# Cross-attention of a fused decoder layer: the SyncE queue takes the softmax denominators before the next keys, and the first pass puts its wide maximum pairs in two banks of the scores

## The reference

```python
q_hk = (hidden_q @ Wq.T).reshape(Bv, Sv, H, K)
q_big = jnp.einsum('bshk,hkq->bshq', q_hk, w_kc_q)
q_big = _apply_rope(q_big, sin_q[None, :, None, :], cos_q[None, :, None, :])
kv_r = _apply_rope(kv_c, sin_k[None], cos_k[None])
q_r = jnp.einsum('bshq,hqr->bhsr', q_big, W_qr)
k_r = jnp.einsum('bld,hdr->bhlr', kv_r, W_kr)
scores = jnp.einsum('bhsr,bhlr->bhsl', q_r, k_r)
attn = jax.nn.softmax(scores, axis=-1)
ctx_c = jnp.einsum('bhsl,bld->bhsd', attn, kv_r)
ctx_lat = jnp.einsum('bhsd,hkd->bhsk', ctx_c, w_kc_kv)
ctx = ctx_lat.transpose(0, 2, 1, 3).reshape(Bv, Sv, H * K)
return ctx @ Wo.T
```

## Time and profile before

| | |
|---|---|
| median of 3 runs | 2580.51 us (2574.94 to 2581.4) |
| the profiled execution | 2568.1 us, its span 2566.3 us |
| mean granted TensorE clock over the span | 0.961 |
| busy over the span | PE 2317.2 us (90%), PEld 1447.2 us (56%), DVE 1686.8 us (66%), ACT 1189.1 us (46%), POOL 1839.7 us (72%) |
| PE busy in 40 slices of the span, tenths | 7989858999985999999999999999999999999398 |
| PEclk in the same slices | 9999978999996999999999999999999999999699 |

### The profile page before, as it was taken

The page is one execution under the profiler, slowest core; times in us unless marked ns, Lnnn a source line. Parts: engine busy times, 40 slices in busy tenths (PEclk is TensorE's granted clock), DMA queues, the critical chain, the costliest instruction groups (busy, mean ns, idle before and its releaser), DMA issues. The chain is left out here.

```text
span 2566.3 us, 47308 instructions
## 1 busy us (share of the span) xinstructions
PE 2317.2 (90%) x15394; PEld 1447.2 (56%) x15394; DVE 1686.8 (66%) x2816; ACT 1189.1 (46%) x1925; POOL 1839.7 (72%) x827
## 2 busy tenths in 40 slices
PE   7989858999985999999999999999999999999398
PEld 4455446777752555555555555555555555555288
DVE  6888857888855666666666666666666666661475
ACT  3232222232222555655655655655655655664143
POOL 2445526989871888888888788888888888889111
PEclk9999978999996999999999999999999999999699
DMA  4000016666654233333333333333333332320111
GB/s 132 14 24 20 13 51 179 185 175 181 177 161 94 64 78 72 85 80 70 83 75 71 86 70 76 86 73 73 86 75 72 86 77 69 86 64 20 39 45 39
DMA packets 229954, 212.21 MB, mean 83 GB/s; under 512 B 115542, under 2 KB 204842, under 8 KB 229760
## 3 DMA queue, kind: packets, MB, share of 16 engines
q1 hardware_dynamic: 229888, 211.37, 32.5%
HBM read 128.17 MB, written 59.48 MB: 73 GB/s over the span
## 5 line engine op out<-in xcount | busy, mean ns | idle before, releaser
L1670 POOL TENSOR_TENSOR x_acc<-x_acc,x_prob 120x1600 f32<-120x1600 f32 (+1 forms) x320 | 1151.4, 3598 | 54.9 <-ACT x_prob L1691 34.2
L1691 ACT ACTIVATE x_prob<-x_scores 120x800 f32<-120x800 f32 (+1 forms) x768 | 601.5, 836 | 19.3 <-PE x_scores L1864 12.3
L1884 PE MATMUL x_context<-x_prob,x_kv 120*64 120x400 f32 (+1 forms) x3072 | 605.7, 515 | 0.0
L1785 DVE TENSOR_REDUCE x_mx<-x_ring 115x2 f32<-115x1024 f32 (+1 forms) x352 | 431.5, 1226 | 52.8 <-PE x_ring L1927 35.3
L1711 ACT COPY x_half<-x_ring 115x420 f32<-115x420 f32 (+2 forms) x320 | 171.5, 536 | 403.4 <-PE x_ring L1934 403.4
L1794 DVE TENSOR_REDUCE x_mx<-x_ring 115x1 f32<-115x420 f32 (+2 forms) x320 | 197.8, 618 | 222.2 <-PE x_ring L1934 222.2
L1884 PEld LDWEIGHTS x_context<-x_prob,x_kv 120*64 120x64 f32 (+1 forms) x3072 | 187.2, 136 | 260.9 <-issue 260.4
L1864 PE MATMUL x_scores<-x_qh,x_dh 64*120 64x400 f32 (+1 forms) x1536 | 274.0, 352 | 1.0 <-ACT x_prob L1691 0.2
L1864 PE MATMUL x_scores<-x_ql,x_dh 64*120 64x400 f32 (+1 forms) x1536 | 266.7, 342 | 0.0
L1864 PE MATMUL x_scores<-x_qh,x_dl 64*120 64x400 f32 (+1 forms) x1536 | 266.5, 342 | 0.0
L1670 POOL TENSOR_TENSOR x_acc<-x_prob 121x1600 f32<-121x1600 f32 x32 | 115.5, 3609 | 173.3 <-ACT x_prob L1691 173.3
(11 more groups left out here) (176 smaller groups left out, 3659.2 us busy)
## 6 DMA issues: line engine op xcount, KB each, us to landing
x_rden<-scratch_rden SPq DMA_DIRECT2D x68, 200.0 KB, 3.5
scratch_qh<-q_qsh SPq DMA_DIRECT2D x64, 200.0 KB, 3.9
scratch_ql<-q_qsl SPq DMA_DIRECT2D x64, 200.0 KB, 3.8
x_qm<-scratch_qh SPq DMA_DIRECT2D x64, 200.0 KB, 4.2
x_qh<-scratch_qh SPq DMA_DIRECT2D x64, 200.0 KB, 3.4
x_ql<-scratch_ql SPq DMA_DIRECT2D x64, 200.0 KB, 3.8
scratch_kr<-q_krot SPq DMA_DIRECT2D x32, 363.0 KB
x_kr<-scratch_kr SPq DMA_DIRECT2D x32, 363.0 KB
```

Of the source, the lines that this page charges most:

```text
L1670: pool.tensor_tensor(acc[0:rows, parity], first, prob[0:rows, c % PR], ALU.add).then_inc(acc_done.sem, 1)
L1691: act.activation(prob[0:rows, c % PR, u * HALF:(u + 1) * HALF].rearrange("p (j s) -> p j s", j=2), psc[0:rows, u, :, 0:BANK], ACT.Exp).the ...
L1785: dve.tensor_reduce(best[0:block_rows(r), :, r, i], ring[0:block_rows(r), :, 0:b - a], AX.X, ALU.max).then_inc(read_sem(u), 1)
L1884: mm = pe.matmul(pav[DC * s:DC * s + DC, j, 0:BANK], kv[0:rows, parity, c], prob[0:rows, c % PR, cols], start=c == 0, stop=c == LC - 1)
```

## The change

There are two parts.

In SyncE's queue `invert(n)` moves ahead of `load_kr(n + 2)`, in all slots that load keys (-1 to 29); `load_qm` stays in front of both. In the other slots nothing changes.

In the first pass the wide pairs go to `psc[:, 0]`, banks 2 and 3 in the numbering of the new `cells`, instead of the ring. `earlier` takes the banks from `cells` and looks back over up to two slots. Two waits are added: the scores of step 0 in slot 0 wait for the last wide maximum of the first pass, and in the first pass the wide pairs with i == 2 (steps 5 to 11), which read the last third of the keys, wait for turn 2. The output product of the first pass takes one head pair instead of eight.

```diff
@@ -1311,6 +1311,10 @@
         self.first = self.count(first, {})
         self.count([u for n, u in last_units], self.last_where, last_units)
 
+    def cells(self, n, u):
+
+        return (2, 3) if u[0] == "max" and is_at(n, -1) else self.banks[u]
+
     def reader(self, u):
         return 2 if u[0] == "max" else self.banks[u][0]
 
@@ -1344,17 +1348,21 @@
     def earlier(self, n, u):
 
         found, seen = [], []
-        for b in self.banks[u]:
+        for b in self.cells(n, u):
             if isinstance(n, int) and n >= self.last:
                 keys = [(self.last - 1, v) for v in self.units] + list(self.last_where)
                 place = keys.index((n, u))
                 m, v = next(key for key in reversed(keys[:place]) if b in self.banks[key[1]])
+            elif isinstance(n, int):
+                keys = [(m, v) for m in (n - 2, n - 1, n) for v in self.units]
+                place = keys.index((n, u))
+                m, v = next((key for key in reversed(keys[:place]) if b in self.cells(*key)), (None, None))
             else:
                 place = self.units.index(u)
                 before = [(0, v) for v in self.units[:place]]
                 back, v = next(key for key in reversed([(1, v) for v in self.units] + before) if b in self.banks[key[1]])
                 m = n - back
-            if v not in seen:
+            if v not in seen and v is not None:
                 seen.append(v)
                 found.append(self.release(m, v))
         return found
@@ -1610,8 +1618,10 @@
                     store_x2(n - 2, parity)
                 if further:
                     load_qm(n + 2, parity)
+                    invert(n)
                     load_kr(n + 2)
-                invert(n)
+                else:
+                    invert(n)
                 if not last:
                     double_steps(n + 1, 1 - parity)
                     load_m(n + 1, 1 - parity)
@@ -1782,7 +1792,8 @@
                 u = ("max", r, i)
                 wait_filled(dve, n, u)
                 a, b = keys_of(r, i)
-                dve.tensor_reduce(best[0:block_rows(r), :, r, i], ring[0:block_rows(r), :, 0:b - a], AX.X,
+                src = psc[:, 0] if is_at(n, -1) else ring
+                dve.tensor_reduce(best[0:block_rows(r), :, r, i], src[0:block_rows(r), :, 0:b - a], AX.X,
                                   ALU.max).then_inc(read_sem(u), 1)
 
             def half_maximum(n, u):
@@ -1855,6 +1866,8 @@
                 cols = slice(u * BANK, (u + 1) * BANK)
                 halves = [slice(DC * j, DC * j + DC) for j in range(2)]
                 pe.wait_ge(exp_done.sem, exp_done.at(n, 2 * c + u - 1))
+                if is_at(n, 0) and c == 0 and u == 0:
+                    wait_read(pe, n - 1, last_max)
                 if c == 0 and u == 0:
                     pe.wait_ge(q_loaded.sems[parity], q_loaded.done(n, parity))
                     pe.wait_ge(steps_doubled.sems[parity], steps_doubled.done(n, parity))
@@ -1914,17 +1927,21 @@
                         mm = pe.matmul(ring[DC * s:DC * s + DC, bank, 0:BANK], ones[0:LP], acc[:, 1 - parity, cols],
                                        start=True, stop=True)
                 elif u[0] == "out":
-                    for h in range(H // 2):
+                    heads = H // 2 if not is_at(n, -1) else 1
+                    for h in range(heads):
                         if h % 4 == 0:
                             wait(pe, ctx_normed.sem, ctx_normed.at(n, h // 4 + 1))
                         mm = pe.matmul(ring[0:S, bank, 0:E], ctxn[:, h // 4, (h % 4) * S:(h % 4 + 1) * S],
-                                       wco[:, h], start=h == 0, stop=h == H // 2 - 1)
+                                       wco[:, h], start=h == 0, stop=h == heads - 1)
                 elif u[0] == "max":
                     r, i = u[1:]
                     a, b = keys_of(r, i)
+                    dst = psc[:, 0] if is_at(n, -1) else ring
+                    if is_at(n, -1) and i == 2:
+                        wait_read(pe, n, ("turn", 2))
                     for t in range(2):
                         part = slice(DC * t, DC * t + DC)
-                        mm = pe.matmul(ring[0:block_rows(r), t, 0:b - a],
+                        mm = pe.matmul(dst[0:block_rows(r), t, 0:b - a],
                                        qm[part, 1 - parity, r * MR:r * MR + block_rows(r)], kh[part, a:b],
                                        start=True, stop=True)
                 elif u[0] == "half":
```

## The result

The changed kernel takes **2492.88 us** (median; 2489.71 to 2493.34), the kernel before 2578.84 in the same comparison: a ratio of 0.9665, 95% interval 0.9649 to 0.9682, so 86 us less. 2505 had been forecast, with a range from 2495: the time lies 12 us under the forecast and 2 under the range. The profiled execution took 2489.7 us, span 2487.9. Trace against trace the spans differ by 2566.3 - 2487.9 = 78.4 us, close to the 75 of the sum.

A forecast was written before the change was run, and what follows sets the result against it. VectorE's wait for the denominators, which holds up TensorE's wide pairs in slots 0 to 29, was taken as the bound. 61 + 14 = 75 us off the median 2580.5 gave 2505; forecast's own range 2498 to 2517, wider range 2495 to 2530.

The forecast's parts named there:

- the 75 of the sum: Whole kernel: 61 us from the queue order plus 14 from the first pass, off the profiled execution's 2568.1 us.
- Part 1, 61 us: Slots 0 to 29: denominators ahead of the key loads in SyncE's queue end VectorE's wait, saving 61 us.
- the lower bound of 54: Slots 0 to 29: least gain of the queue order, 30 x (1.54 idle + 0.25 restart) = 54 us.
- Part 2, 14 us: First pass: wide pairs in idle score banks and a one-head output product save 14 us, between 10 and 16.
- its bound of 16: First pass: upper gain, 11.9 us from reductions without alternating plus 4.6 from the shorter output product, given as 16.
- 3.0 less 0.9 for the clock: First pass's output product: 3.0 of 4.6 us saved are kept, less 0.9 for slot 0 starting at low clock.
- Late keys, late doubled steps: Slots: keys and `x_dl` land later behind the moved wait, with 6.7 us left for `x_dl`; cost put at nothing.
- GpSimd did not take over: Rival, 13%: in the slots, GpSimd's normalised context comes late and the output product waits, 25 us in all; about 2530.
- The queue order did not backfire: Rival, 4%: `x_dl` lands over 6.7 us later than worked out, next slot's scores wait; each us beyond costs 30.
- the first pass gave more than forecast and not little: Rival, 15%: first pass gives little or a small new wait stays in slots, worth 5 to 12 us; about 2515.
- the change does what it says: Opposing rival, 3%: denominators in the slots are late for another reason and only the first pass gains; 2566.
- The step that failed: Whole kernel: the profiled execution lay 12.4 us below the median, so 75 was taken off 2580.5, giving 2505.

The follow-up runs named there:

- the one matmul for two: The changed kernel with one matmul of 128 columns per bank instead of two of 64 for the first pass's denominators: 2492.63 us, ratio 0.9679.
- five stores: The changed kernel with the denominators stored five times instead of once, each store waited for: 2614.53 us, ratio 1.0162 to the kernel before.

## Why the prediction was wrong

Point by point:

- **What bounds the kernel, and the place of the edit:** right. Both ways to bring the denominators in time (queue order, reciprocal one step later) end the stall and give 57 and 58 us. The prediction did not see that moving the reader alone would do. (The slot that it calls 12 is number 11 in its own count of slots 0 to 29.)
- **Part 1, 61 us:** 60.6 from trace to trace, and 62.4 counted from the first use of the maxima. The runs with this part or its equal alone gave 57.0 and 57.8. In the three traces of the kernel before the excess per slot is 1.66 to 2.02 us, 50 to 61 in all, so its size depends on which execution one has profiled; the lower bound of 54 held for the runs and not for every trace. Slots take 46.2 to 46.3 us (slot 0: 46.6), as forecast.
- **Part 2, 14 us:** 17.3 (51.58 us from the first half pair to the first use of the maxima became 34.29), above its bound of 16 (its terms, 11.9 + 4.6, make 16.5), and 17.0 by itself. The residual sum that ends the pass comes 18.1 us earlier, 15 to 16 had been forecast. Mis-sized was "Between two reductions with nothing to wait for it loses about 0.02 us [...]; I take 0.04". Back to back they gain 0.08 to 0.09 each instead, and the two stretches came out 3.2 us shorter than worked out (8.19 for 9.3, 15.80 for 17.9). The trace from before had shown it: the reciprocal of the earlier trace rows ends at 1391.51, and the reduction behind it starts at 1391.43. Of the product's 4.6 us, 2.3 were gained (6.99 to 4.70), where 3.0 less 0.9 for the clock, 2.1, had been taken. The size is right and its parts are not: the maxima came later than the 4.0 us after the product's start that had been taken, since their store's round trip took 1.2 us longer, and the low clock lay mostly ahead of the 0.56 us in which TensorE waits for them. With the old queue order, 3.15 us were gained, at the low clock and with no wait. The page of the Trainium skill that was cited there ("TensorE: Matmul & The Clock Gate", Part 1) states that the default state is throttled and that activity releases it. The traces agree: behind the product with one head slot 0 is granted 0.97 and takes 46.6 us, behind eight heads 1.00 and 45.5.
- **Late keys, late doubled steps, put at nothing:** right in the slots. In the first pass TensorE waits 0.28 us for `x_dl`, and the maxima come some 0.9 us later than with the old order (4.70 against 3.84 us behind the product's start). The sentence that the store of the maxima "depends on the end of the slot and not on the queue" holds for its issue and not for its round trip.
- **The rivals:** GpSimd did not take over: in slot 10 the first half of the normalised context is ready at about 1315.95, the product starts at 1316.67, so 0.7 us were left and nothing waited. The queue order did not backfire, the first pass gave more than forecast and not little, the reciprocal delays no step (3.23 us from half pair to half pair), and the change does what it says.
- **The sum, 75 us off the profiled execution, 2493:** the changed kernel's profiled execution took 2489.7, 3.4 less. That its median is 2492.9 is luck, since a sum off the profiled execution says nothing of the median; and the parts measured alone, 57 and 17 for 61 and 14, show that two errors cancel in the sum. **The step that failed** is the one behind it: "That execution was 12.4 us below the median of the runs shown; off the median, 2580.5 - 75". It carries the 12.4 us over to the changed kernel, as if they were time that the edit leaves alone. The changed kernel's own profiled execution is 3.2 below its median. The miss of 12.6 us is these 12.4 - 3.2 = 9.2 and 78.4 - 75 = 3.4 from the sum.

What the runs showed in its place: the kernel before has medians of 2578.8, 2564.9, 2563.8 and 2572.4 us in four comparisons, the changed one 2492.9 and 2489.3 (and 2492.6 in the fourth, with the one matmul for two). So the gain is 86 us where the kernel before stands at 2579, 80 where it stands at 2572 and 75 where it stands at 2564: most of what varies between comparisons goes with the edit, and the 12.4 us were not to be carried over whole. The right base was either the profiled execution, or the median with a sum that grows with it.

Where in the kernel it goes is shown in part. The first trace has 10.8 us more than the second in slots 0 to 29, in longer waits of the stall and in more slots at the low clock, and the edit removes both; where a late reader is made on purpose and worse (five stores), low-clock slots multiply. But no trace is of an execution near 2579, and the other phases of the kernel vary by some 4 us too, so that the 10 us above the profiled execution lie in the stall is inferred, not seen. The spread within a comparison points the same way, but roughly, and over unequal numbers of runs: about 3 us for each of the two kernels that end the stall by one edit (5 runs each) and 4 to 8 for the changed one (4 and 5), but 10.6 with the old queue order (6) and 10 to 12 for the kernel before where 9 to 17 runs were made; with 4 it was 6.5.

What stays open: why the waits are longer in the first trace of the kernel before than in the two later ones, and why its medians differ. Whether it is the chip was not separated: the three later comparisons ran on three different chips.

## What to carry to other kernels

Where the profiled execution and the median of the runs differ, ask which wait could hold the difference before adding it to the forecast: if it is the wait that the edit removes, part or all of it goes as well, and the sum belongs to the profiled execution. In a queue that is served in order, what a computing engine waits for goes ahead of what is read much later; letting the reader come one step later was worth the same here. A transfer that is moved back can still lengthen a round trip behind it: look at what is then under way. A stall costs more than its idle time once TensorE's clock falls after it.

## What the hardware showed that had not been expected

VectorE's reductions back to back start 0.08 to 0.09 us ahead of the recorded end of the one before, for lengths of 0.6 and of 1.2 us. The round trip of the denominators' store took 1.66 to 1.72 us with no key loads just ahead and 2.61 behind three of them; that of the maxima's store 1.34 us, and 1.92 to 2.65 with the doubled steps issued some 4 us ahead of it. Idle times of TensorE of 0.76 us in the mean left its clock alone in slots 1 to 29 (granted 1.00 each); of 1.34 to 1.54 us, 1 to 4 of these 29 slots grew by 1.5 us or more, at 0.97; of 2.3 us, 16 did. Two matmuls with 64 columns of weights on the two halves of the array took no longer together than one with 128 (2.94 us for four such pairs, 3.04 for four of 128).
